# Flamingo layer on one Trainium2 core: combinations of x made from x before it is split, low parts of x on GpSimd, all value tiles ahead of the first query products

## The chip, the cores and the metric

The kernel runs on one core of a Trainium2 chip. The time is the device time of one execution in microseconds. A core has five engines, each with its own in-order queue: PE (TensorE), ACT (ScalarE), DVE (VectorE), POOL (GpSimd) and SP (SyncE, which here only issues DMAs). Each waits at an instruction until the semaphores that it names have reached their values.

## The reference, cut to what matters

Eight sequences of 128 tokens of width 512 and a context of the same shape go through two gated layers. The change concerns the first attention, with 32 heads of width 128:

```python
x = x + tanh(g_xattn[0]) * L0_xattn(layernorm(x), ctx, mask, bias, ln_weight, w_q, w_k, w_v, w_out)
...
xn = rmsnorm(hidden) * ln_weight
h_q, h_k, h_v = xn @ w_q.T, ctx @ w_k.T, ctx @ w_v.T
score = softmax(where(mask, h_q @ h_k.T + position_bias, -inf))
out = hidden + (score @ h_v) @ w_out.T
```

A linear layer, a second attention and an expert layer follow, which the change leaves alone.

## The kernel before

**Precision.** Every large product is made of three passes. A factor is split in a high part, rounded to the fast matmul type (fp32r), and a low part, which is the factor minus its high part; high times high, high times low and low times high are added up in PSUM. So each operand exists twice in SBUF. ACT writes the high part (`ACT.Copy` into an fp32r tile), DVE or POOL then subtracts it.

**Groups.** The 32 heads go in 8 groups of 4. Group 0 ("first") is written out by hand; groups 1 to 7 are a loop and a last body. In the loop, queries and keys are made by a Strassen-like scheme with seven products (`P1` to `P7`), which need *combinations* of the activations: T1, T2, T3 and N4, sums and differences of the blocks `x_block(i, s)` of x (i is the half of the width, s the half of the tokens) and of the same blocks `c_block` of the context. There are four combinations of each, every one split into high and low. They are made once, during group 0, in the tiles `work[0..3]`, written to DRAM (`combined`, by `put`), and fetched into a ring of places by the loop. Group 0 itself makes queries and keys plainly (`plain("q0a")`: head 0, tokens 0 to 511; `b`: the other half).

**Where x comes from.** DVE writes the normalised x (L1339). PE transposes it by sequence (`x_transposed`, L1861) into banks 4 to 7. Before the change ACT makes the high part out of PSUM, scaled by the norm weight, in four instructions of 128x128 for each sequence (`x_hi`, L964), and DVE the low part, again four (L1345). A combination of x is made from both parts of its blocks (`combine_x`, L1477, ten instructions of 128x1024 on DVE; `combine_context`, L1453, seven on DVE, and L663, three on POOL). `combined_hi` (ACT, L978) and `combined_lo` (POOL, L673) split each one. Combinations of the context come first, those of x after them, between softmax work.

**The order of the work.** Each engine's block is a list written by hand. PE's list in group 0, after the first keys, is: values 0 to 2 (`value`, L1937), x_transposed 0 to 3, value 3, x_transposed 4 to 7, the four query products of heads 0 and 1 (L1897), `scores` of head 0 (L1954), values 4 to 7, scores of head 1, keys of heads 2 and 3, `attend(0, 0)` (L1970), queries q2a, q2b, q3a, `attend(0, 1)`, q3b, scores of head 2, output projections (`project`, L1998). `UNITS` numbers all these tiles of work; four PSUM banks are given round by that number, so a tile waits until the one four places earlier has been emptied.

**The softmax** of a head runs DVE, ACT, DVE: `softmax_in` adds `bm` (made by POOL's `biasmask`, L682) to the scores in PSUM and takes the negative maximum (L1374, L1376), `exps` on ACT (L952), `softmax_out` scales and transposes (L1396, L1400). `scores` of head 1 waits until L1396 of head 0 has read each bank. SP then sends the turned probabilities to DRAM (`passed`) and back (`back`, into `keyed`), and `attend` waits for that. SP's DMAs stand in one queue.

`plain_hi` (ACT) and `plain_lo` (POOL) split the weights of the plain products; `plain_out` (ACT, L893) and `value_out` (ACT, L945) empty banks. `scores` of head 0 waits for `plain_out("q0b")`. L1352 to L1359 on DVE make the scaled x in `acc`, to which the outputs are added.

## Time and profile before

| | |
|---|---|
| median of 3 runs | 959.33 us (958.12 to 960.22) |
| profiled execution, its own time | 959.01 us |
| its span in the profile | 957.2 us |
| PE busy | 941.9 us, 98% of the span |
| DVE, ACT, POOL busy | 594.2, 399.5, 497.3 us |
| chain that ended last | PE 78%, DVE 8%, DMA 7% |

The profiled execution lies 0.3 us under the median. "Busy" is the time with an instruction on the engine. PE is busy nearly all the time, so time can only be won or lost where PE stands still, and group 0 takes the first 135 us of the span.

### The profile page before, as it was taken

The numbers are of one execution on the slowest core, as the hardware profiler recorded it, in microseconds if no ns is written. First come the engines' busy times: TensorE is split into PE (matmuls) and PEld (weight loads), VectorE is DVE, ScalarE is ACT, GpSimd is POOL, SyncE is SP. The second block draws the span as 40 slices with busy tenths as digits, with TensorE's granted clock in tenths as the row PEclk, the third lists the DMA queues.
The fourth block names the chain that finished last, engine by engine and source line by source line (L and its number), as shares of the span: only waits on it lengthen the run. The fifth ranks groups of instructions, "written<-read, shape, count | busy, mean of one in ns | idle before, by whom it ended". The sixth has DMA issues, their size and how long they took to land.

```text
span 957.2 us, 15391 instructions
## 1 busy us (share of the span) xinstructions
PE 941.9 (98%) x4850; PEld 793.9 (83%) x4850; DVE 594.2 (62%) x1020; ACT 399.5 (42%) x1080; POOL 497.3 (52%) x463
## 2 busy tenths in 40 slices
PE   9999899999999999999999999999999999999998
PEld 8888688788888888888888888888888888888885
DVE  4888846385538553855486447654666966756754
ACT  5765424252434233433443333433443346646630
POOL 3756754454446453646374637463646336687530
PEclk9999999999999999999999999999999999999999
DMA  7145676775687567766777667767687665200002
GB/s 283 45 152 222 234 255 249 259 266 196 241 276 275 219 241 263 271 244 241 251 271 256 241 241 260 270 248 237 226 292 266 230 224 183 91 23 1 2 1 88
DMA packets 67380, 199.44 MB, mean 208 GB/s; under 512 B 8720, under 2 KB 21264, under 8 KB 66320
## 3 DMA queue, kind: packets, MB, share of 16 engines
q1 hardware_dynamic: 66336, 197.67, 57.4%
q10 hardware_dynamic: 1008, 1.32, 0.4%
q8 instruction: 19, 0.31, 0.1%
q14 instruction: 17, 0.14, 0.0%
HBM read 174.85 MB, written 24.12 MB: 208 GB/s over the span
## 4 chain that ended last, share of the span: by engine, by line
PE 78%; DVE 8%; DMA 7%; issue 2%; SPq 2%; ACT 1%; POOL 1%; DVEq 0%; ACTq 0%
PE bank L1921 23%; PE bank L1998 16%; PE bank L2102 10%; PE bank L1937 10%; DMA keyed<-passing 6%; PE bank L1970 6%; PE bank L1954 5%; PE bank L1897 3%; PE bank L2126 2%; DVE turned_blocks L1396 1%; SPq L442 1%; DVE kt L1436 1%; DVE turned_blocks L1400 1%; PE bank L1982 1%; PE bank L2255 1%
## 5 line engine op out<-in xcount | busy, mean ns | idle before, releaser
L1998 PE MATMUL bank<-wvo,ao 128*128 128x512 f32 x768 | 179.9, 391 | 0.7 <-issue 0.6
L1937 PE MATMUL bank<-wvo,ct 128*128 128x512 f32 x768 | 177.7, 390 | 0.0
L1998 PEld LDWEIGHTS bank<-wvo,ao 128*128 128x128 f32 x768 | 143.0, 188 | 30.1 <-issue 1.0
L1937 PEld LDWEIGHTS bank<-wvo,ct 128*128 128x128 f32 x768 | 143.5, 188 | 29.3
L603 POOL TENSOR_TENSOR wvo<-stage,wvo 128x512 fp32r<-128x512 f32 x64 | 85.4, 1357 | 148.4 <-ACT wvo L906 148.3
L1921 PE MATMUL bank<-ring,wkq 128*128 128x512 f32 x648 | 157.4, 390 | 0.0
L1921 PEld LDWEIGHTS bank<-ring,wkq 128*128 128x128 f32 x648 | 121.2, 188 | 25.1
L1414 DVE SCALAR_TENSOR_TENSOR acc<-bank,gated_rows,acc 128x512 f32<-128x512 f32 x128 | 93.2, 742 | 39.4 <-PE bank L1998 38.3
L952 ACT ACTIVATE bank<-bank,nmax 128x128 f32<-128x128 f32 x256 | 88.2, 351 | 55.6 <-DVE nmax L1376 55.6
L1405 DVE TENSOR_TENSOR ao<-bank,ao 128x512 fp32r<-128x512 f32 x64 | 43.9, 691 | 106.6 <-ACT ao L958 106.6
L1436 DVE TENSOR_TENSOR qt<-bank,qt 128x512 f32<-128x512 f32 x98 | 66.4, 690 | 57.4 <-PE bank L1921 56.0
L682 POOL TENSOR_TENSOR bm<-maskneg,bias 128x1024 f32<-128x1024 f32 x32 | 78.9, 2465 | 26.0 <-DVE bank L1374 26.0
L945 ACT ACTIVATE vals<-bank 128x512 f32<-128x512 f32 x64 | 38.4, 600 | 94.7 <-PE bank L1937 94.4
L623 POOL TENSOR_TENSOR wkq_raw<-stage 128x256 f32<-128x256 f32 x27 | 20.3, 754 | 110.7 <-PE bank L1921 102.2
L1436 DVE TENSOR_TENSOR kt<-bank,kt 128x512 f32<-128x512 f32 x91 | 60.4, 682 | 26.6 <-PE bank L1921 25.0
L958 ACT ACTIVATE ao<-bank 128x512 fp32r<-128x512 f32 x64 | 37.9, 599 | 80.7 <-PE bank L1970 79.0
L1970 PEld LDWEIGHTS bank<-keyed,vals 128*128 128x128 f32 x512 | 61.0, 191 | 12.7 <-DMA keyed<-passing 11.1
L1970 PE MATMUL bank<-keyed,vals 128*128 128x128 f32 x512 | 63.6, 277 | 5.7 <-DMA keyed<-passing 5.6
L1374 DVE TENSOR_TENSOR bank<-bank,bm 128x512 f32<-128x512 f32 x64 | 44.4, 694 | 37.3 <-PE bank L1954 36.4
L1921 PE MATMUL bank<-xb,wkq 128*128 128x512 f32 x252 | 65.5, 395 | 0.0
L649 POOL TENSOR_TENSOR wkq<-wkq_raw,wkq 128x1024 fp32r<-128x1024 f32 x27 | 65.2, 2414 | 0.0
L1954 PEld LDWEIGHTS bank<-kt,qt 128*128 128x128 f32 x512 | 62.1, 191 | 3.4 <-DVE turned_blocks L1396 0.9
(187 smaller groups left out, 1511.9 us busy)
## 6 DMA issues: line engine op xcount, KB each, us to landing
ring<-combined SPq DMA_DIRECT2D x216, 512.0 KB, 6.3
stage<-in_w SPq DMA_DIRECT2D x63, 512.0 KB, 4.2
passing<-turned_blocks SPq DMA_DIRECT2D x24, 512.0 KB, 2.9
keyed<-passing SPq DMA_DIRECT2D x96, 128.0 KB, 3.2
combined<-work SPq DMA_DIRECT2D x16, 512.0 KB, 3.6
xraw<-in_x SPq DMA_DIRECT2D x2, 1024.0 KB, 11.3
bias<-in_bias SPq DMA_DIRECT2D x8, 256.0 KB, 4.5
cs<-in_ctx SPq DMA_DIRECT2D x1, 2048.0 KB, 7.8
```

The costliest lines, as they stand in the source:

```text
L603: pool.tensor_tensor(wvo[:, 1, h, :], stage[:, vo_stage(g, m, c)[0], :], wvo[:, 0, h, :].bitcast(fp32), ALU.subtract).then_inc(s_vo_lo, 1)
L649: pool.tensor_tensor(wkq[:, 3:7, 1, :, :].rearrange("p k c d -> p k (c d)"), wkq_raw[:, 3:7, 1, :, :].rearrange("p k c d -> p k (c d)"), w ...
L682: pool.tensor_tensor(bm[:, :, :], maskneg[:, :, :], bias[:, h:h + 1, :].to_broadcast([P, B, P]), ALU.add).then_inc(s_bm, 1)
L952: act.activation(scores, scores, ACT.Exp, bias=nmax[:, b:b + 1], accum_out=esum[:, b:b + 1]).then_inc(s_exp, 1)
L1414: dve.scalar_tensor_tensor(out=acc[:, b, :], in0=bank[un_of[m][f"o{i}"] % RING if to is None else to][:, :], scalar=gated_rows[:, b:b + 1] ...
L1436: dve.tensor_tensor(dst, bank[un_of[m][f"{ADDED[step]}.{j}"] % RING][:, :], other, ALU.add).then_inc(s_add, 1)
L1921: mm = pe.matmul(bank[b][:, :], wkq[:, FACTOR[p], w, c, :], right(s), start=(c == 0 and w + s == 0), stop=(c == 1 and w == 1))
L1937: mm = pe.matmul(bank[un_of[m][u] % RING][:, :], ct[:, i, c, b * P:(b + 1) * P], wvo[:, j, c, :], start=(c == 0 and i + j == 0), stop=(c = ...
L1954: mm = pe.matmul(bank[4 + s][:, (b - 4 * s) * P:(b - 4 * s + 1) * P], qt[:, h % 2, b * P:(b + 1) * P], kt[:, h % 2, b * P:(b + 1) * P], st ...
L1970: mm = pe.matmul(bank[6 + s][:, (b - 4 * s) * P:(b - 4 * s + 1) * P], vals[:, b, h * P:(h + 1) * P], right, start=True, stop=True)
L1998: mm = pe.matmul(bank[to][:, :], ao[:, h, p, b * P:(b + 1) * P], wvo[:, j, 2 * pair + h, :], start=(h == 0 and p + j == 0), stop=(h == 1 a ...
L2102: mm = pe.matmul(bank[b][:, 0:n], left(i, c), right[:, j, c, :], start=(c == 0 and i + j == 0), stop=(c == KC - 1 and i == 1 and last))
```

## The change

**x.** DVE copies the transposed x times the norm weight whole, in fp32, into the place of the low part (`x_raw`; two instructions of 128x256 for each sequence). ACT makes the high part from it in SBUF. DVE makes the four combinations from the whole x, four instructions in place of ten, and the low parts of the first two of them; then POOL subtracts the high part in place, so that the block holds the low part (`x_lo`, four instructions of 128x1024). **Context.** Its ten instructions all stand on DVE; POOL's three are gone. Combinations of x now come first. **Order.** Values 4 to 7 stand ahead of the query products, whose first now waits for three `x_lo` and the third for all four. Keys of heads 2 and 3 stand before and after scores of head 1, q2a ahead of `attend(0, 0)`. The raw x is loaded into `acc` itself.

```diff
-MAKING = ["T1", "T2", "N4", "T3"]
+MAKING = {1: ["T1", "T3", "T2", "N4"], 0: ["T1", "T2", "N4", "T3"]}
+X_STEPS = 6
...
-UNITS = {"first": (PLAIN_UNITS[0:4] + VALUES[0:4] + PLAIN_UNITS[4:8] + VALUES[4:8] + PLAIN_UNITS[8:16] + OUTS[:B]
+UNITS = {"first": (PLAIN_UNITS[0:4] + VALUES + PLAIN_UNITS[4:16] + OUTS[:B]
                    + PLAIN_UNITS[16:20] + OUTS[B:]),
...
+    xb_raw = nc.alloc_sbuf_tensor_at("xb_raw", [P, 3, 2, 2, H], fp32, offset=xr_at)
+    x01_raw = nc.alloc_sbuf_tensor_at("x01_raw", [P, 2, 2, H], fp32, offset=ring_at)
+    def x_raw(i, s):
+        return x01_raw[:, 1, :, :] if (i, s) == (0, 1) else xb_raw[:, {(0, 0): 0, (1, 0): 1, (1, 1): 2}[i, s], 1, :, :]
...
+    xraw = acc
...
-                def put(z, i, w):
-                    t = MAKING[i]
-                    sp.wait_ge(s_comb_lo, 4 * z + i + 1)
+                def put(z, i):
+                    t = MAKING[z][i]
+                    if z == 1 and i < 2:
+                        sp.wait_ge(s_comb, 4 + i + 1)
+                    else:
+                        sp.wait_ge(s_comb_lo, (i - 1 if z == 1 else 2 + i + 1))
                     for c in range(2):
+                        sp.dma_start(combined[z, TS.index(t), c, :, :, :], work[i][:, c, :, :].bitcast(fp32)).then_inc(s_cin[4 * z + i], 16)
...
                 sp.wait_ge(s_plain_lo, 4)
                 load(0, "q2", 0)
+                for i in range(4):
+                    put(1, i)
+                put(0, 0)
+                put(0, 1)
                 sp.wait_ge(s_plain_lo, 6)
                 load(0, "o0", 1)
                 passed(0, 0)
+                put(0, 2)
                 back(0, "first", 0)
-                put(0, 0, 0)
-                put(0, 1, 1)
-                put(0, 2, 2)
+                put(0, 3)
                 passed(0, 1)
                 back(0, "first", 1)
-                put(0, 3, 3)
                 sp.wait_ge(s_vo_lo, 6)
...
+                def x_lo(i, s):
+                    pool.wait_ge(s_xhi, 2 * (HB * s + HB))
+                    pool.wait_ge(s_comb, {(0, 0): 1, (0, 1): 2, (1, 1): 3, (1, 0): 4}[i, s])
+                    pool.tensor_tensor(x_block(i, s)[:, 1, :, :], x_raw(i, s),
+                                       x_block(i, s)[:, 0, :, :].bitcast(fp32), ALU.subtract).then_inc(s_xlo, 1)
...
+                def combined_lo(z, i):
+                    pool.wait_ge(s_comb_hi, 4 * (1 - z) + i + 1)
                     if z == 1:
-                        pool.wait_ge(s_comb, 7 + (4, 6, 7, 10)[i])
+                        pool.wait_ge(s_comb, 4)
                     elif i < 2:
-                        pool.wait_ge(s_comb, (1, 3)[i])
+                        pool.wait_ge(s_comb, X_STEPS + (4, 6)[i])
+                    pool.tensor_tensor(work[i][:, :, 1, :], work_raw[i][:, :, 1, :],
+                                       work[i][:, :, 0, :].bitcast(fp32), ALU.subtract).then_inc(s_comb_lo, 1)
...
+                for i, s in ((0, 0), (0, 1), (1, 0), (1, 1)):
+                    x_lo(i, s)
+                combined_lo(1, 2)
+                combined_lo(1, 3)
                 plain_lo(4)
+                combined_lo(0, 0)
+                combined_lo(0, 1)
                 biasmask(0, 1)
                 plain_lo(5)
-                pool.wait_ge(s_comb, 4)
-                combined_lo(0, 0, 0)
-                combined_lo(0, 1, 1)
-                combined_lo(0, 2, 2)
+                combined_lo(0, 2)
                 plain_lo(6)
+                combined_lo(0, 3)
                 plain_lo(7)
-                combined_lo(0, 3, 3)
...
-                    act.wait_ge(s_xT, b + 1)
...
+                    act.wait_ge(s_xraw, B + 2 * b + 2)
+                    for i in range(2):
+                        t = slice(b % 4 * P, (b % 4 + 1) * P)
+                        act.activation(x_block(i, b // 4)[:, 0, :, t], x_raw(i, b // 4)[:, :, t], ACT.Copy).then_inc(s_xhi, 1)
+                def combined_hi(z, i):
+                    act.wait_ge(s_comb, i + 1 if z == 1 else X_STEPS + (3, 5, 7, 10)[i])
+                    act.activation(work[i][:, :, 0, :], work_raw[i][:, :, 1, :], ACT.Copy).then_inc(s_comb_hi, 1)
...
                 for b in range(4, B):
                     x_hi(b)
+                value_out(0, "first", 4)
+                combined_hi(1, 0)
+                combined_hi(1, 1)
+                value_out(0, "first", 5)
+                combined_hi(1, 2)
+                combined_hi(1, 3)
+                value_out(0, "first", 6)
                 plain_hi(4)
-                for u in ("q0a", "q1a", "q0b", "q1b"):
-                    plain_out(u)
-                combined_hi(0, 0, 0)
+                value_out(0, "first", 7)
+                plain_out("q0a")
+                plain_out("q1a")
+                combined_hi(0, 0)
+                plain_out("q0b")
+                combined_hi(0, 1)
+                plain_out("q1b")
+                plain_hi(5)
                 exps(0, 0, [0])
-                value_out(0, "first", 4)
+                plain_out("k2a")
                 exps(0, 0, [1])
-                plain_hi(5)
-                value_out(0, "first", 5)
-                value_out(0, "first", 6)
-                combined_hi(0, 1, 1)
-                value_out(0, "first", 7)
-                combined_hi(0, 2, 2)
+                combined_hi(0, 2)
+                plain_out("k2b")
                 plain_hi(6)
                 exps(0, 1, [0])
-                plain_out("k2a")
+                plain_out("k3a")
                 exps(0, 1, [1])
-                plain_out("k2b")
+                combined_hi(0, 3)
                 plain_hi(7)
                 vo_hi(0, "first", "o0")
                 vo_hi(0, "first", "o1")
-                plain_out("k3a")
                 plain_out("k3b")
-                combined_hi(0, 3, 3)
+                plain_out("q2a")
...
+                dve.wait_ge(s_const, 32)
                 for b in range(B):
-                    dve.wait_ge(s_xhi, b * KC + KC)
-                    for c in range(KC):
-                        dve.scalar_tensor_tensor(out=x_block(c // 2, b // 4)[:, 1, c % 2, b % 4 * P:(b % 4 + 1) * P],
-                                                 in0=bank[4 + b % 4][:, c * P:(c + 1) * P], scalar=cols[:, 0, c:c + 1],
-                                                 in1=x_block(c // 2, b // 4)[:, 0, c % 2, b % 4 * P:(b % 4 + 1) * P].bitcast(fp32),
-                                                 op0=ALU.mult, op1=ALU.subtract).then_inc(s_xlo, 1)
+                    dve.wait_ge(s_xT, b + 1)
+                    for i in range(2):
+                        dve.tensor_tensor(x_raw(i, b // 4)[:, :, b % 4 * P:(b % 4 + 1) * P],
+                                          bank[4 + b % 4][:, i * 256:i * 256 + 256].rearrange("p (c t) -> p c t", c=2),
+                                          cols[:, 0, 2 * i:2 * i + 2].unsqueeze(2).to_broadcast([P, 2, P]),
+                                          ALU.mult).then_inc(s_xraw, 1)
+                dve.wait_ge(s_xraw, B + 2 * B)
+                t1, t3, t2, n4 = (work_raw[w][:, :, 1, :] for w in range(4))
+                dve.tensor_tensor(t1, x_raw(0, 1), x_raw(0, 0), ALU.subtract).then_inc(s_comb, 1)
+                dve.tensor_tensor(t3, x_raw(1, 1), x_raw(0, 1), ALU.subtract).then_inc(s_comb, 1)
+                dve.wait_ge(s_comb, 1)
+                dve.tensor_tensor(t2, x_raw(1, 1), t1, ALU.subtract).then_inc(s_comb, 1)
+                dve.wait_ge(s_comb, 3)
+                dve.tensor_tensor(n4, x_raw(1, 0), t2, ALU.subtract).then_inc(s_comb, 1)
+                for i in range(2):
+                    dve.wait_ge(s_comb_hi, i + 1)
+                    dve.tensor_tensor(work[i][:, :, 1, :], work_raw[i][:, :, 1, :], work[i][:, :, 0, :].bitcast(fp32),
+                                      ALU.subtract).then_inc(s_comb, 1)
                 dve.tensor_reduce(gated_rows[:, :], maskf[:, :, :], AX, ALU.max).then_inc(s_mf, 1)
...
+                combine_context([0, 1, 2, 3, 4, 5, 6])
                 softmax_in(0, 0)
                 softmax_out(0, "first", 0, 0)
                 softmax_out(0, "first", 0, 1)
-                combine_context([0, 1, 2, 3])
+                combine_context([7, 8, 9])
                 softmax_in(0, 1)
                 softmax_out(0, "first", 1, 0)
                 softmax_out(0, "first", 1, 1)
-                combine_context([4, 5, 6])
                 ao_lo(0, 0)
-                combine_x([0, 1, 2, 3, 4])
                 ao_lo(0, 1)
                 softmax_in(0, 2)
...
-                        pe.wait_ge(s_xlo, (b - 3) * KC)
+                        pe.wait_ge(s_xraw, B + 2 * (b - 3))
...
                 for x in range(4, B):
                     x_transposed(x)
-                pe.wait_ge(s_xlo, 4 * KC)
-                plain("q0a")
-                plain("q1a")
-                pe.wait_ge(s_xlo, B * KC)
-                plain("q0b")
-                plain("q1b")
-                scores(0, "first", 0)
                 for b in range(4, B):
                     value(0, "first", b)
+                for s in range(2):
+                    pe.wait_ge(s_xlo, 3 + s)
+                    plain("q0" + "ab"[s])
+                    plain("q1" + "ab"[s])
+                scores(0, "first", 0)
+                plain("k2a")
+                plain("k2b")
                 scores(0, "first", 1)
-                for u in PLAIN_UNITS[8:12]:
-                    plain(u)
+                plain("k3a")
+                plain("k3b")
+                plain("q2a")
                 attend(0, 0)
-                plain("q2a")
                 plain("q2b")
```

The places at which the lists differ and of which the prediction speaks follow. In brackets stand the semaphores waited for.

DVE before, from the end of the low parts of x to the first softmax (`gated_rows`, `rscale`, `vsum`, `msq` are small tiles, `bank` the scores of head 0):

```order
L1345 SCALAR_TENSOR_TENSOR xb<-bank,cols,xb 128x128 x2
L1349 TENSOR_REDUCE gated_rows<-maskf 128x8
L1352 TENSOR_SCALAR rscale<-rstd,tg 128x8 [waits act_prep]
L1354 SCALAR_TENSOR_TENSOR vsum<-mv,rscale 128x8 [waits rms_steps]
L1356 TENSOR_SCALAR msq<-rscale 128x8
L1359 TENSOR_SCALAR acc<-xraw,msq,vsum 128x512 [waits rms_steps]
L1359 TENSOR_SCALAR acc<-xraw,msq,vsum 128x512 x7
L1362 TENSOR_SCALAR gated_rows<-gated_rows,tg 128x8 [waits mask_steps]
L1374 TENSOR_TENSOR bank<-bank,bm 128x512 [waits biasmask_done,scores_done,layernorm_x,mask_steps]
L1376 TENSOR_REDUCE nmax<-bank 128x4 [waits scores_read]
```

DVE after the change, from the last `x_raw` tile on; `work_raw_96` to `work_raw_99` are the whole combinations T1, T3, T2 and N4 of x, `ctx_hi` is the semaphore that now counts `x_raw`:

```order
L1347 TENSOR_TENSOR work_raw_96<-x_raw,xb_raw 128x2x512 [waits ctx_hi]
L1348 TENSOR_TENSOR work_raw_97<-xb_raw,x_raw 128x2x512
L1350 TENSOR_TENSOR work_raw_98<-xb_raw,work_raw_96 128x2x512 [waits combine_steps]
L1352 TENSOR_TENSOR work_raw_99<-xb_raw,work_raw_98 128x2x512 [waits combine_steps]
L1355 TENSOR_TENSOR work_92<-work_raw_96,work_92 128x2x512 [waits combined_hi]
L1355 TENSOR_TENSOR work_93<-work_raw_97,work_93 128x2x512 [waits combined_hi]
L1357 TENSOR_REDUCE gated_rows<-maskf 128x8
L1360 TENSOR_SCALAR rscale<-rstd,tg 128x8 [waits act_prep]
L1362 SCALAR_TENSOR_TENSOR vsum<-mv,rscale 128x8 [waits rms_steps]
L1364 TENSOR_SCALAR msq<-rscale 128x8
L1367 TENSOR_SCALAR acc<-acc,msq,vsum 128x512 [waits rms_steps]
L1367 TENSOR_SCALAR acc<-acc,msq,vsum 128x512 x7
```

And directly behind these, on DVE after the change, up to the first softmax (`ct` is the context; the `work_raw` tiles are used again):

```order
L1370 TENSOR_SCALAR gated_rows<-gated_rows,tg 128x8 [waits mask_steps]
L1461 TENSOR_TENSOR work_raw_96<-ct 128x2x512 [waits ctx_in4,layernorm_x,mask_steps]
L1461 TENSOR_TENSOR work_raw_96<-work_raw_96,ct 128x2x512 [waits combine_steps] x2
L1461 TENSOR_TENSOR work_raw_97<-ct,work_raw_96 128x2x512 [waits combine_steps,ctx_in5]
L1461 TENSOR_TENSOR work_raw_97<-work_raw_97,ct 128x2x512 [waits combine_steps]
L1461 TENSOR_TENSOR work_raw_98<-ct,work_raw_97 128x2x512 [waits combine_steps,ctx_in6]
L1461 TENSOR_TENSOR work_raw_98<-work_raw_98,ct 128x2x512 [waits combine_steps]
L1382 TENSOR_TENSOR bank<-bank,bm 128x512 [waits scores_done,biasmask_done]
```

Where L1349 came directly behind the low parts, six instructions of 128x1024 now stand before it, and seven more of the context between the scaled x and the first softmax.

ACT before and after, from the fifth weight split to the first exponential (`qt` is a query tile emptied, `work` a high part of a combination, `vals` a value tile):

```order
L886 ACTIVATE wplain<-stage 128x512 [waits plain_done,stage_in1]
L893 ACTIVATE qt<-bank 128x512 [waits plain_done] x4
L978 ACTIVATE work_91<-work_raw_95 128x2x512 [waits pool_prep]
L952 ACTIVATE bank,esum<-bank,nmax 128x128 [waits negmax_done]
L952 ACTIVATE bank,esum<-bank,nmax 128x128 x3
L945 ACTIVATE vals<-bank 128x512 [waits values_done]
```

```order
L946 ACTIVATE vals<-bank 128x512 [waits values_done]
L894 ACTIVATE qt<-bank 128x512 [waits plain_done] x2
L971 ACTIVATE work_92<-work_raw_96 128x2x512 [waits combine_steps]
L894 ACTIVATE qt<-bank 128x512 [waits plain_done]
L971 ACTIVATE work_93<-work_raw_97 128x2x512 [waits combine_steps]
L894 ACTIVATE qt<-bank 128x512 [waits plain_done]
L887 ACTIVATE wplain<-stage 128x512 [waits plain_done,stage_in1]
L953 ACTIVATE bank,esum<-bank,nmax 128x128 [waits negmax_done]
```

The four `qt` stood together; now the third and fourth each stand behind a high part of a context combination, which waits for DVE's `combine_steps`.

POOL before, from the first `bm`, and after the change, behind it (`xb` and `x_61` are blocks of x, `wplain` weights):

```order
L682 TENSOR_TENSOR bm<-maskneg,bias 128x1024 [waits scores_read,bias_in]
L663 TENSOR_TENSOR work_raw_95<-ct 128x2x512 [waits x_transposed]
L663 TENSOR_TENSOR work_raw_95<-work_raw_95,ct 128x2x512 [waits pool_prep] x2
L597 TENSOR_TENSOR wplain<-stage,wplain 128x512 [waits plain_weights_hi]
L682 TENSOR_TENSOR bm<-maskneg,bias 128x1024 [waits scores_read]
L597 TENSOR_TENSOR wplain<-stage,wplain 128x512 [waits plain_weights_hi]
```

```order
L675 TENSOR_TENSOR xb<-xb_raw,xb 128x1024 [waits combine_steps,x_hi]
L675 TENSOR_TENSOR x_61<-x_raw,x_61 128x1024 [waits combine_steps,x_hi]
L675 TENSOR_TENSOR xb<-xb_raw,xb 128x1024 [waits combine_steps,x_hi] x2
L686 TENSOR_TENSOR work_94<-work_raw_98,work_94 128x2x512 [waits combine_steps,combined_hi]
L686 TENSOR_TENSOR work_95<-work_raw_99,work_95 128x2x512 [waits combine_steps,combined_hi]
L609 TENSOR_TENSOR wplain<-stage,wplain 128x512 [waits plain_weights_hi]
L686 TENSOR_TENSOR work_92<-work_raw_96,work_92 128x2x512 [waits combine_steps,combined_hi]
```

Three instructions that read the context went; four `x_lo` and two low parts of x combinations stand in their place, and each waits for DVE's combining.

## Rows read from the trace of the kernel before

**Rows 1.** What PE waited for in the first 160 us: total, times, longest, in us.

```profile
PE bank L1982 <- DVE ao L1405: 2.3, 1, 2.3
PE bank L1970 <- DMA keyed<-passing: 1.1, 1, 1.1
...
PE bank L1954 <- DVE turned_blocks L1396: 0.7, 1, 0.7
```

**Rows 2.** The page's TensorE clock, granted tenths in 40 slices of the span.

```profile
PEclk9999999999999999999999999999999999999999
```

**Rows 3.** PE in order of time: start, us, line, operation, tiles, count, idle before.

```profile
31.28 1.91 PE L1861 MATMUL bank<-ident,craw 128*128 128x128 f32 x16
...
37.52 0.63 PE L1861 MATMUL bank<-ident,craw 128*128 128x128 f32 x4 [0.27 <-DVE xb L1345]
...
50.61 11.14 PE L1937 MATMUL bank<-wvo,ct 128*128 128x512 f32 x48
...
61.59 1.95 PE L1954 MATMUL bank<-kt,qt 128*128 128x128 f32 x16
...
63.29 11.14 PE L1897 MATMUL bank<-ct,wplain 128*128 128x512 f32 x48
...
84.26 1.95 PE L1970 MATMUL bank<-keyed,vals 128*128 128x128 f32 x16
...
90.85 8.42 PE L1998 MATMUL bank<-wvo,ao 128*128 128x512 f32 x36
...
108.69 2.05 PE L1970 MATMUL bank<-keyed,vals 128*128 128x128 f32 x16 [1.14 <-DMA keyed<-passing]
```

**Rows 4.** DVE in order of time: low parts of x, context and x combinations.

```profile
33.14 4.22 DVE L1345 SCALAR_TENSOR_TENSOR xb<-bank,cols,xb 128x128 fp32r<-128x128 f32 x16 [1.46 <-ACT xb L964]
...
61.17 1.23 DVE L1453 TENSOR_TENSOR work_raw<-work_raw,ct 128x1024 f32<-128x1024 f32 x1
...
78.24 1.84 DVE L1477 TENSOR_TENSOR work_raw<-x,xb 128x1024 f32<-128x1024 f32 x1
...
80.12 2.21 DVE L1477 TENSOR_TENSOR work_raw<-work_raw,x 128x1024 f32<-128x1024 f32 x1
...
82.36 2.22 DVE L1477 TENSOR_TENSOR work_raw<-work_raw,xb 128x1024 f32<-128x1024 f32 x1
```

**Rows 5.** POOL in order of time, beside the same stretches.

```profile
62.47 7.10 POOL L673 TENSOR_TENSOR work<-work_raw,work 128x1024 fp32r<-128x1024 f32 x3 [4.94 <-DVE work_raw L1453]
...
78.95 4.55 POOL L603 TENSOR_TENSOR wvo<-stage,wvo 128x512 fp32r<-128x512 f32 x2
...
83.45 3.37 POOL L682 TENSOR_TENSOR bm<-maskneg,bias 128x1024 f32<-128x1024 f32 x1
```

**Rows 6.** Line L1359, scaled x in acc on DVE: min/median/max ns.

```profile
L1359 DVE TENSOR_SCALAR acc<-xraw,msq,vsum x8: 531/536/1420, 45.7 to 49.8; 128x512 f32<-128x512 f32 x8
```

**Rows 7.** ACT: the high part of one combination.

```profile
49.60 1.05 ACT L978 ACTIVATE work<-work_raw 128x1024 fp32r<-128x1024 f32 x1
```

**Rows 8.** DVE: first softmax of head 0, first and last of its instructions.

```profile
50.53 0.70 DVE L1374 TENSOR_TENSOR bank<-bank,bm 128x512 f32<-128x512 f32 x1
...
53.75 0.69 DVE L1396 TENSOR_TENSOR turned_blocks<-bank,rinv 128x512 f32<-128x512 f32 x1
...
55.87 0.69 DVE L1396 TENSOR_TENSOR turned_blocks<-bank,rinv 128x512 f32<-128x512 f32 x1
...
56.59 0.71 DVE L1400 STREAM_TRANSPOSE turned_blocks<-turned_blocks 128x512 f32<-128x512 f32 x1
```

**Rows 9.** SP: probabilities of heads 0 and 2 out and back.

```profile
57.93 0.43 SPq L432 DMA_DIRECT2D passing<-turned_blocks  x1
...
62.99 2.52 SPq L442 DMA_DIRECT2D keyed<-passing  x4
...
101.63 0.32 SPq L432 DMA_DIRECT2D passing<-turned_blocks  x1
...
104.28 1.74 SPq L442 DMA_DIRECT2D keyed<-passing  x4
```

85 lines of the change are left out of this document (8 added, 77 removed).

## The prediction

> **What bounds the kernel now.** PE is busy for 98% of the span, so I first asked what PE waits for in group 0, the only part that the change touches. The waits of PE in the first 160 us [rows 1] are 2.3 us for `ao_lo` of head 2 ahead of the transposes, 1.1 us for its probabilities coming back, and 0.7 us for the softmax of head 2 ahead of `scores` of head 3. All lie behind 99 us. Ahead of them PE waits 0.27 us for a low part of x [rows 3]. So the change can win at most 2.3 + 1.1 + 0.7 + 0.3 = 4.4 us, or 4.6 with the issue time beside the last; whatever it loses, it loses by making PE stand still.
>
> Then I looked at what DVE and POOL do to each other. One DVE instruction with two SBUF operands of 128x1024 takes 1.23 us when POOL is idle (second of [rows 4]). From 78.24 us on, three such take 1.84, 2.21 and 2.22 us, while POOL's pair of 128x512 at 78.95 takes 4.55 us and its `bm` at 83.45 takes 3.37 us [rows 4, 5]. Undisturbed, POOL needs 7.10/3 = 2.37 us for 128x1024 [rows 5], about 1.3 us for half of it. The ends tell how they share: DVE's second instruction ends at 82.33, which is 80.12 + about 1.1 us of waiting for POOL's first half + 1.15 of its own; POOL's second half then ends at 83.50, 1.2 us behind. 4.55 = 2 x 1.28 + 2 waits of 1.0. **They take turns, one whole instruction each, and neither overlaps.** A scaled-x instruction of L1359 falls under it too: seven took about 0.53 us, one 1.42 us [rows 6]. Instructions that read scores or products from PSUM do not: POOL's three of 2.37 us at 62.47 [rows 5] ran through a softmax of DVE undelayed.
>
> On this the change bears hard: it puts six POOL instructions of 128x1024 and one of 128x512 beside DVE's combining and scaling, all ahead of the first softmax.
>
> **The change part by part**, against the profiled execution's 959.01 us (0.3 us under the median of 959.33).
>
> *PE up to the first query.* x is transposed from 31.28 us; four tiles take 1.67 us, value 3 2.74. Without the wait of 0.27 us and the like amount behind it, PE ends the transposes at 37.4 in place of 37.9: gain 0.5. Values 4 to 7 (10.98 us from 50.61 to 61.59 [rows 3]) now follow, to 48.4.
>
> *DVE's whole x.* Sixteen instructions of 128x256 from PSUM, a form that the trace lacks: above 4.22/16 = 0.26 us for 128x128 [rows 4], under 0.69 for 128x512 [rows 8]. I take 0.36, by size. The last four tiles come off PE from 36.5 to 37.7, so DVE ends at about 39.3 (38.4 and 42 at the bounds). ACT's high parts follow within 0.7 us.
>
> *DVE against POOL, by turns,* with 1.15 us for a DVE turn, 2.3 for a POOL turn of 128x1024, 1.25 for one of 128x512:
> - T1 39.4 to 40.6; T3 to 41.8 (it waits for nothing); `x_lo` 1 to 44.1; T2 to 45.2; `x_lo` 2 to 47.5; N4 to 48.7; DVE's first low part to 49.8; `x_lo` 3 to 52.1; second low part to 53.2; `x_lo` 4 to 55.5.
> - Small ones to 55.6; `combined_lo` of x to 57.9 and 60.3 with one scaled-x instruction between or behind; `plain_lo(4)` to 62; the rest of the eight, at 0.47 each, to 65.3 (the eight span 45.7 to 50.3 with 0.9 of waiting [rows 6]).
> - Context steps at 1.26 each (1.23 plus the semaphore): the third, T1, done at 69.3, the fourth at 70.6; then turns again with POOL's two low parts, the seventh done at 76.6, or 78.9 if POOL wins one draw.
>
> If POOL did not hold up DVE, the same DVE list would end its third context step at 56.0 and its seventh at 61.
>
> *What PE loses by it.* First, q0a needs `x_lo` 3: 52.1 against 48.4, **3.7**. The four query products (10.9 us) end at 63.0; the fourth `x_lo` is in time. Second, `scores` of head 0 needs `plain_out("q0b")`, which on ACT stands behind `combined_hi(0, 0)`; that waits for the third context step, 69.3, takes 1.0 [rows 7], and the copy 0.5: 70.9, **7.9**. With scores (1.70) and k2a, k2b (5.45) PE is at 78.1. Third, `scores` of head 1 waits until L1396 of head 0 has read each bank. From `softmax_in` to these ends are 3.9 and 6.0 us (50.53 to 54.44 and 56.56 [rows 8]), so 80.5 and 82.6: **2.4** and **1.3**. PE leaves scores 1 at 83.5. Fourth, head 0's softmax ends 6.8 us behind its start [rows 8], 83.3; T3 of the context takes three DVE turns beside two of POOL's, to 89.8; softmax of head 1 starts there; its exponentials end near 94.9 (5.1 us in, ahead of the second L1396), and only then ACT splits T3 (95.8), POOL its low part (98.2) and the weights of q3 (99.5). PE, through k3a, k3b, q2a, `attend(0, 0)` and q2b, stands at q3a at 96.1 or, with head 0's probabilities late by a us, 97.4; it starts at 99.5: **2 to 3.4**. Fifth, SP sends head 1's probabilities behind `put(0, 3)`, at 99.0. A round trip took 7.1 us with nothing in front (101.63 to PE's start at 108.69), but 5.1 rather than 2.7 to the second half with a load in front (57.93 to 62.99) [rows 3, 9]. I take 5.2 + 4.4: PE starts `attend(0, 1)` at 108.6; it was ready at 102.3. **6.3**, or 3.8 with the short trip.
>
> Before, `attend(0, 1)` started at 84.26 [rows 3]: 24.3 us later. From there PE's list is the same as before; the projections, which began at 90.85 [rows 3], follow. The five combining instructions of x that stood between the softmax of heads 2 and 3 are gone from DVE and their halves from ACT and POOL, so the waits of 2.3, 1.1 and 0.7 us should go [rows 1]: -4.1. SP's fetches for the loop come as early as before, counted from there, and the loop is untouched. Sum: 24.3 - 4.1 = 20.2; 959.0 + 20.2 = **979.2**.
>
> The Trainium skill (SBUF — State Buffer, "Who interferes with whom") names `tensor_scalar` among the operations that can take both port pairs, if operands allow. The trace has it in one instruction of eight. If the eight did not wait, DVE's chain would be 4 us shorter and the sum 975.
>
> **The rivals.**
> 1. *No turns: the lists run as the durations say.* For it: not one row of before has DVE in the new `x_raw` form, and `x_lo` writes in place. Against it: rows 4 and 5. Then `x_lo` 3 is done at 47, the third context step at 56.0, PE waits nowhere up to q2b. SP still sends head 1's probabilities only at 80.7. With the long trip PE waits 6.4 for `attend(0, 1)`, starting it at 90.3 in place of 84.26, and ends at 959.0 + 6.0 - 4.1 = 961; with the short one at 958.4; if they come back by 83.5, when PE is ready, only the gains are left: 959.0 - 0.5 - 4.1 = 954.4. It decides where `x_lo` 3 ends before 48.4.
> 2. *The turns hold, but the queues behind them clear.* The first three losses stand (15.3 in all), head 1 comes in time: 959.0 + 15.3 - 0.5 - 4.1 = 969.7. For it: that part rests on the longest chain of my estimates.
> 3. *PE's clock falls after the long waits.* The granted clock shows 9 tenths or more in all 40 slices, with no wait over 2.3 us [rows 1, 2]; here are waits of 8 and 6 us. At 1.2 in place of 2.4 GHz, 128x512 at 0.23 us (10.98/48) would take twice that. Behind the 7.9 us the next wait swallows it; behind the last one `attend` and q3b (4.4 us) would be paid twice: 979.2 + 4.4 = 983.6. The Trainium skill (TensorE: Matmul & The Clock Gate) says that waits between bursts of matmuls can let the clock fall; no row here shows it.
>
> **How the numbers follow.** Forecast, 971 to 982 (the draw on POOL's side adds 2.3; the short trip, the undelayed scaling and the smaller `x_raw` take off 2.5, 4 and 1): 0.60. Rival 2, with the same spread, 963 to 971: 0.22. Rival 3: 0.05. Rival 1: 0.13, of which 0.07 under 957.1, 0.04 within 0.2% (957.4 to 961.2, about what a measurement can tell from no change), 0.02 above. So faster 0.08, same 0.04, slower 0.88. The range that holds 8 in 10 leaves out rival 1 and reaches up to rival 3: 963 to 984.
>
> **What would show it.** Right: on DVE, T2, N4 and the second low part at about 3.4 us each; PE waiting 3 to 4 us ahead of q0a for `x_lo`, and about 8 ahead of the first scores for ACT's q0b; the first softmax at 75 to 79 us; no wait ahead of the transposes of head 2. Wrong: DVE's combinations at 1.2 us beside `x_lo`; or PE at q0a by 48.5; or the losses there and the end at 960, which would mean that a later stage gives them back.

## The result and the profile after

| | before | after |
|---|---|---|
| median | 958.73 us (957.88 to 960.22, 4 runs) | 979.48 us (978.57 to 980.24, 4 runs) |
| profiled execution, its span | 959.01, 957.2 us | 980.24, 978.3 us |
| mean granted clock | 1.0 | 0.989 |
| PE, DVE, ACT, POOL busy | 941.9, 594.2, 399.5, 497.3 us | 949.9, 596.0, 395.8, 494.3 us |

The ratio is 1.0208 (95%: 1.0191 to 1.0226): slower by 20.7 us. The forecast was 979.2. DVE and POOL are busy for as long as before, though DVE has 17 instructions less (1003 for 1020) and the loop is the same. An instruction that waits for its turn counts as busy, and the rows below show that what the combinations save goes into such waits.

The waits of PE in the first 180 us of the kernel after, which answer to [rows 1]:

```profile
PE bank L1947 <- DMA keyed<-passing: 6.9, 2, 4.7
PE bank L1931 <- ACT qt L894: 5.2, 1, 5.2
PE bank L1874 <- POOL xb L675: 3.1, 1, 3.1
PE bank L1931 <- DVE turned_blocks L1404: 1.1, 2, 0.7
...
PE bank L1959 <- DVE ao L1413: 0.2, 1, 0.2
```

L1947 is `attend`, L1931 `scores`, L1874 the plain products, L1959 the transposes. The old waits of 2.3, 1.1 and 0.7 us have shrunk to 0.2; new ones of 16.3 stand ahead of them. PE's timeline, against [rows 3]:

```profile
37.54 11.13 PE L1914 MATMUL bank<-wvo,ct 128*128 128x512 f32 x48
51.72 7.36 PE L1874 MATMUL bank<-xb,wplain 128*128 128x512 f32 x24 [3.05 <-POOL xb L675]
...
69.72 3.57 PE L1931 MATMUL bank<-kt,qt 128*128 128x128 f32 x16 [5.20 <-ACT qt L894]
73.04 5.73 PE L1874 MATMUL bank<-ct,wplain 128*128 128x512 f32 x24
79.20 1.13 PE L1931 MATMUL bank<-kt,qt 128*128 128x128 f32 x8 [0.43 <-DVE turned_blocks L1404]
80.99 1.16 PE L1931 MATMUL bank<-kt,qt 128*128 128x128 f32 x8 [0.67 <-DVE turned_blocks L1404]
...
92.54 3.02 PE L1947 MATMUL bank<-keyed,vals 128*128 128x128 f32 x16 [2.19 <-DMA keyed<-passing]
...
106.41 3.79 PE L1947 MATMUL bank<-keyed,vals 128*128 128x128 f32 x16 [4.71 <-DMA keyed<-passing]
109.85 1.94 PE L1874 MATMUL bank<-x,wplain 128*128 128x512 f32 x6
...
114.71 8.42 PE L1975 MATMUL bank<-wvo,ao 128*128 128x512 f32 x36
...
154.32 1.52 PE L1898 MATMUL bank<-xb,wkq 128*128 128x512 f32 x6
```

Read as a ledger against before: `attend(0, 1)` starts at 106.41 in place of 84.26 (+22.15), the projections at 114.71 in place of 90.85 (+23.9), the loop at 154.32 in place of 135.06 (+19.3), and the span is 21.1 longer. So 22.15 are lost ahead of `attend(0, 1)`, 1.7 in it and in the work up to the projections, 4.6 come back behind it, and 1.8 are lost from the loop to the end. Of the 22.15, 16.3 are the waits above; the other 6 or so are PE's own work, which runs at the lower clock behind some of them (the first 24 query matmuls take 7.36 us, before 5.73). The 1.8 are no more than that stretch scatters by itself: from the start of the loop to the end, the traces of all kernels of this document but the last one take 819.4 to 824.0 us, before 822.1 and after 824.0.

DVE from the end of x_raw to the first softmax (L1347 T1, L1348 T3, L1350 T2, L1352 N4, L1355 two low parts, L1367 the scaled x, L1461 context steps, L1382 `softmax_in`):

```profile
39.28 1.23 DVE L1347 TENSOR_TENSOR work_raw<-x_raw,xb_raw 128x1024 f32<-128x1024 f32 x1
40.43 1.22 DVE L1348 TENSOR_TENSOR work_raw<-xb_raw,x_raw 128x1024 f32<-128x1024 f32 x1
41.56 3.43 DVE L1350 TENSOR_TENSOR work_raw<-xb_raw,work_raw 128x1024 f32<-128x1024 f32 x1
45.02 3.31 DVE L1352 TENSOR_TENSOR work_raw<-xb_raw,work_raw 128x1024 f32<-128x1024 f32 x1
48.26 4.49 DVE L1355 TENSOR_TENSOR work<-work_raw,work 128x1024 fp32r<-128x1024 f32 x2
...
53.80 1.20 DVE L1360 TENSOR_SCALAR rscale<-rstd,tg 128x8 f32<-128x8 f32 x1
55.04 2.31 DVE L1362 SCALAR_TENSOR_TENSOR vsum<-mv,rscale 128x8 f32<-128x8 f32 x1
...
57.47 6.70 DVE L1367 TENSOR_SCALAR acc<-acc,msq,vsum 128x512 f32<-128x512 f32 x8
...
65.60 2.49 DVE L1461 TENSOR_TENSOR work_raw<-work_raw,ct 128x1024 f32<-128x1024 f32 x2
...
70.78 3.20 DVE L1461 TENSOR_TENSOR work_raw<-ct,work_raw 128x1024 f32<-128x1024 f32 x1
...
75.16 0.69 DVE L1382 TENSOR_TENSOR bank<-bank,bm 128x512 f32<-128x512 f32 x1
```

and POOL beside it (L675 `x_lo`, L686 `combined_lo`):

```profile
40.65 3.25 POOL L675 TENSOR_TENSOR xb<-xb_raw,xb 128x1024 fp32r<-128x1024 f32 x1 [3.37 <-DVE work_raw L1347]
43.86 3.40 POOL L675 TENSOR_TENSOR x<-x_raw,x 128x1024 fp32r<-128x1024 f32 x1
48.48 6.50 POOL L675 TENSOR_TENSOR xb<-xb_raw,xb 128x1024 fp32r<-128x1024 f32 x2 [1.23 <-DVE work_raw L1352]
54.94 4.74 POOL L686 TENSOR_TENSOR work<-work_raw,work 128x1024 fp32r<-128x1024 f32 x2
```

The rows show the turns: T1 and T3 at 1.2 us each, T2 and N4 at 3.43 and 3.31, a low part at about 1.2 and the next at 3.3. `x_lo` takes 3.25 to 3.40 where POOL needs 2.37 alone [rows 5].

### The profile page after: what moved, and what is told of

It is laid out like the page before. It is cut to its first block, busy times and chain, and to the rows that moved or that the text cites. A ratio compares the mean times of both kernels' runs of the same rounds, so it can differ in the third digit from the quotient of the medians.

```text
span 978.3 us, 15359 instructions
## 1 busy us (share of the span) xinstructions
PE 949.9 (97%) x4850; PEld 800.7 (82%) x4850; DVE 596.0 (61%) x1003; ACT 395.8 (40%) x1064; POOL 494.3 (51%) x462
## 4 chain that ended last, share of the span: by engine, by line
PE 74%; DMA 8%; DVE 7%; issue 2%; SPq 2%; ACT 1%; POOL 0%; DVEq 0%; ACTq 0%
PE bank L1898 23%; PE bank L1975 15%; PE bank L2080 10%; PE bank L1914 9%; PE bank L1947 6%; DMA keyed<-passing 6%; PE bank L1931 5%; PE bank L2104 2%; DVE work_raw L1461 1%; SPq L456 1%; DMA passing<-turned_blocks 1%; DVE turned_blocks L1404 1%; DVE kt L1444 1%; DVE turned_blocks L1408 1%; PE bank L1874 1%
## 5 line engine op out<-in xcount | busy, mean ns | idle before, releaser
L615 POOL TENSOR_TENSOR wvo<-stage,wvo 128x512 fp32r<-128x512 f32 x64 | 82.1, 1303 | 167.1 <-ACT wvo L907 167.1
L695 POOL TENSOR_TENSOR bm<-maskneg,bias 128x1024 f32<-128x1024 f32 x32 | 76.8, 2401 | 20.2 <-DVE bank L1382 20.2
L1947 PEld LDWEIGHTS bank<-keyed,vals 128*128 128x128 f32 x512 | 63.9, 199 | 18.7 <-DMA keyed<-passing 17.0
L1947 PE MATMUL bank<-keyed,vals 128*128 128x128 f32 x512 | 66.7, 286 | 12.1 <-DMA keyed<-passing 11.8
L1931 PEld LDWEIGHTS bank<-kt,qt 128*128 128x128 f32 x512 | 63.5, 196 | 9.7 <-ACT qt L894 5.6
L1931 PE MATMUL bank<-kt,qt 128*128 128x128 f32 x512 | 64.2, 279 | 6.3 <-ACT qt L894 5.2
L1382 DVE TENSOR_TENSOR bank<-bank,bm 128x512 f32<-128x512 f32 x64 | 44.4, 694 | 38.7 <-PE bank L1931 37.7
```

Source lines behind the costliest of these rows:

```text
L615: pool.tensor_tensor(wvo[:, 1, h, :], stage[:, vo_stage(g, m, c)[0], :], wvo[:, 0, h, :].bitcast(fp32), ALU.subtract).then_inc(s_vo_lo, 1)
L695: pool.tensor_tensor(bm[:, :, :], maskneg[:, :, :], bias[:, h:h + 1, :].to_broadcast([P, B, P]), ALU.add).then_inc(s_bm, 1)
L1382: dve.tensor_tensor(scores, scores, bm[:, bs, :], ALU.add).then_inc(s_sadd, 1)
L1931: mm = pe.matmul(bank[4 + s][:, (b - 4 * s) * P:(b - 4 * s + 1) * P], qt[:, h % 2, b * P:(b + 1) * P], kt[:, h % 2, b * P:(b + 1) * P], st ...
L1947: mm = pe.matmul(bank[6 + s][:, (b - 4 * s) * P:(b - 4 * s + 1) * P], vals[:, b, h * P:(h + 1) * P], right, start=True, stop=True)
```

## The experiments

Twelve kernels. "Ratio" is to the kernel before, run on the same chip, with its 95% interval; the kernel after has 1.0208 (1.0191 to 1.0226).

**Does POOL's reading hold up DVE?** In place of four subtractions POOL sets the low parts of x to zero:

```diff
-                    pool.tensor_tensor(x_block(i, s)[:, 1, :, :], x_raw(i, s),
-                                       x_block(i, s)[:, 0, :, :].bitcast(fp32), ALU.subtract).then_inc(s_xlo, 1)
+                    pool.memset(x_block(i, s)[:, 1, :, :].bitcast(fp32), 0.0).then_inc(s_xlo, 1)
```

> The four x_lo subtractions on POOL are replaced by four instructions of POOL that set the low part of x to zero: they write the same tiles and read nothing. This leaves the low part of x out of the query products of group 0 and of the loop. Theory (what DVE takes turns with is POOL's reading of two SBUF operands): T2, N4 and the second low part on DVE take about 1.2 us each in place of 3.3 to 3.4, q0a does not wait, the first softmax starts at about 66 in place of 75.2 us, and the time is 968 to 971. Rival A (any POOL instruction of 128x1024 on SBUF takes a turn, one that only writes as well): DVE's rows stay near 3 us or fall only by what POOL's instruction is shorter, 974 to 978. Rival B (DVE's chain is not what bounds the end): the first softmax is earlier but the time stays above 977.

Measured: 969.9 us, ratio 1.0110 (1.0088 to 1.0132). DVE and POOL of this run:

```profile
42.01 1.22 DVE L1349 TENSOR_TENSOR work_raw<-xb_raw,work_raw 128x1024 f32<-128x1024 f32 x1
43.27 1.22 DVE L1351 TENSOR_TENSOR work_raw<-xb_raw,work_raw 128x1024 f32<-128x1024 f32 x1
...
67.14 0.69 DVE L1381 TENSOR_TENSOR bank<-bank,bm 128x512 f32<-128x512 f32 x1
```

```profile
41.08 0.96 POOL L675 MEMSET xb<- 128x1024 f32 x1 [3.83 <-DVE work_raw L1346]
42.22 0.96 POOL L675 MEMSET x<- 128x1024 f32 x1 [0.18 <-DVE work_raw L1347]
```

T2 runs from 42.01 to 43.23 with POOL's write of 42.22 to 43.18 inside it, and takes 1.22 us. So a POOL instruction that writes the same amount but reads nothing takes no turn, and the first softmax starts 8 us earlier. So what stretched T2 and N4, and with them DVE's list, is that POOL reads. The Trainium skill (SBUF — State Buffer, "Who interferes with whom") says that a DVE instruction with two SBUF inputs contends with a GpSimd instruction that reads SBUF and not with one that only writes; the run agrees.

**Who should make the low parts?** The four subtractions go to DVE, behind N4:

```diff
-                for i, s in ((0, 0), (0, 1), (1, 0), (1, 1)):
-                    x_lo(i, s)
...
+                for i, s in ((0, 0), (0, 1), (1, 0), (1, 1)):
+                    if s == 0 and i:
+                        dve.wait_ge(s_comb, 4)
+                    dve.tensor_tensor(x_block(i, s)[:, 1, :, :], x_raw(i, s),
+                                      x_block(i, s)[:, 0, :, :].bitcast(fp32), ALU.subtract).then_inc(s_xlo, 1)
```

> One part of the change undone: the four low parts of x are made by DVE, behind N4 and ahead of its first combined low part, and not by POOL. Theory (DVE's list with the turns sets the first softmax; one instruction of DVE costs it 1.2 us, one of POOL that takes a turn costs DVE 2.2, but POOL's two combined low parts now come beside the four): the wait of 3.1 us ahead of q0a shrinks to 0 to 1.5, the first softmax still starts at 74 to 76 us, PE waits by so much longer ahead of the scores, and the time stays at 978 to 980. Rival (the wait ahead of q0a counts in full): 976 to 977.

Measured: 975.48 us, ratio 1.0159 (1.0136 to 1.0182): 4.0 us less than after, 4.7 by the ratios, whose intervals do not meet. I had not expected that, and it is not the rival's way either, for q0a waits 3.15 us, as in the kernel after. DVE of this run:

```profile
57.51 0.22 DVE L1364 TENSOR_SCALAR rscale<-rstd,tg 128x8 f32<-128x8 f32 x1
57.76 0.17 DVE L1366 SCALAR_TENSOR_TENSOR vsum<-mv,rscale 128x8 f32<-128x8 f32 x1
...
58.05 3.74 DVE L1371 TENSOR_SCALAR acc<-acc,msq,vsum 128x512 f32<-128x512 f32 x8
...
72.81 0.69 DVE L1386 TENSOR_TENSOR bank<-bank,bm 128x512 f32<-128x512 f32 x1
```

DVE takes on four instructions (4.9 us of its own), and its first softmax still starts 2.35 us earlier. The gain lies in rows that I had held to be small: with POOL silent after 53 us, rscale and vsum, 8 columns each, take 0.22 and 0.17 us where they took 1.20 and 2.31, and the eight scalings 3.74 where they took 6.70. These are 6.1 us of pure waiting in the kernel after; the list ahead of them is 3.6 us longer (from T1 to rscale 18.07 us for 14.52), not 4.9, since the turns fall otherwise there too. A turn costs what is left of POOL's instruction, here up to 2.1 us, however small DVE's own is; the forecast gave the small ones 0.1 us behind the fourth `x_lo`. It also answers the question left open beside rows 6: the eight `tensor_scalar` do wait.

**Do ACT's and SP's places matter?** Two edits of the kernel after. In the first ACT copies q0b, q1b and splits a weight ahead of the first context combinations:

```diff
-                combined_hi(0, 0)
                 plain_out("q0b")
-                combined_hi(0, 1)
                 plain_out("q1b")
                 plain_hi(5)
+                combined_hi(0, 0)
+                combined_hi(0, 1)
```

> Change alone: on ACT, the copies of q0b and q1b and plain_hi(5) stand ahead of the high parts of the first two context combinations. Theory (DVE's list, stretched by the turns with POOL, sets when the first softmax can run; ACT's order only decides where PE waits for it): PE starts the scores of head 0 at about 64.6 us in place of 69.7, and stands still by as much longer ahead of the scores of head 1 or of k2, because the first softmax still starts at about 75 us; the time stays within 1.5 us of the changed kernel's 979.5. Rival (the place of the high parts on ACT is itself the cost): the wait of 5.2 us goes and nothing takes its place, 974 to 975.

Measured: 978.9 us, 1.0195 (1.0176 to 1.0215), no difference from after that the intervals show. PE's wait of 5.20 is gone and one of 9.06 is in its place:

```profile
52.44 5.73 PE L1874 MATMUL bank<-xb,wplain 128*128 128x512 f32 x24 [3.05 <-POOL xb L675]
...
63.45 1.95 PE L1931 MATMUL bank<-kt,qt 128*128 128x128 f32 x16
...
79.91 3.87 PE L1931 MATMUL bank<-kt,qt 128*128 128x128 f32 x16 [9.06 <-DVE turned_blocks L1404]
```

So the 5.2 us that PE's list lays on ACT are DVE's: the last releaser in a row is not always the cause. In the second SP sends head 1's probabilities first:

```diff
-                put(0, 3)
                 passed(0, 1)
+                put(0, 3)
```

> Change alone: SP sends the probabilities of head 1 ahead of the last context combination. Theory (the round trip starts late and is long because the send stands behind two DMAs of 0.5 MB): the probabilities leave at about 94.5 in place of 97.05 us, the trip takes about 7 in place of 9.4 us, and attend(0, 1) starts 2.5 to 4.7 us earlier: 975 to 977. Rival (the trip is not lengthened by what stands ahead of it, or PE only waits elsewhere instead, for the low part that q3a needs): under 1 us, 978.5 to 979.5.

Measured: 976.92 us, 1.0170 (1.0143 to 1.0196). The wait is 3.22 in place of 4.71, `attend(0, 1)` starts at 103.99 in place of 106.41 and the projections at 111.96 in place of 114.71. The time is as forecast, but single runs spread from 973.5 to 978.4, and the interval just touches that of after. The reason given for it held only in half: the probabilities leave at 94.72 in place of 97.05, but their trip takes 9.3 us as before and not 7, for the two stores of the combination now stand between the way out and the way back. What is won is the earlier start alone.

**What does PE's clock cost?** Matmuls whose result nobody reads fill PE's four waits:

```diff
+                def fill(n):
+                    for _ in range(n):
+                        pe.matmul(bank[7][:, 0:P], ident[:, :], ident[:, :], start=True, stop=True)
```

> Adds matmuls of 128x128 whose result nobody reads (12, 20, 7 and 18) in the places where PE waits for the low parts of x, for the scores of head 0, for attend(0, 0) and for attend(0, 1); every wait of the changed kernel stays. Theory (part of the loss is that PE works at the lower granted clock behind its waits): the granted clock stays at 1.00 through the first 120 us, attend(0, 1) with q3b takes 6.1 in place of 8.3 us, and the time falls by 2 to 3 us, to 976.5 to 977.5; what the other stretches at the lower clock cost is hidden by the waits behind them. Rival (the lower clock is hidden by waits everywhere): 979.5, or later by what the added matmuls hold up.

Measured: 977.05 us, 1.0179 (1.0157 to 1.0200), mean clock 1.0 in place of 0.989. First the kernel after, the clock by stretches of 5 us (columns: stretch, length, PE busy, PEclk, DMA share, GB/s):

```profile
50.00:55.00 5.00, 3.28 (x9) 0.75 0.80 325
...
105.00:110.00 5.00, 3.59 (x17) 0.50 0.60 211
200.00:205.00 5.00, 3.78 (x20) 0.76 0.06 18
```

then PE of the run with the filling:

```profile
52.00 5.74 PE L1874 MATMUL bank<-xb,wplain 128*128 128x512 f32 x24 [0.39 <-POOL xb L675]
...
106.35 2.05 PE L1947 MATMUL bank<-keyed,vals 128*128 128x128 f32 x16 [1.46 <-DMA keyed<-passing]
```

The same 24 query matmuls take 5.74 us in place of 7.36, `attend(0, 1)` 2.05 in place of 3.79. `attend(0, 1)` starts at the same time as in after (106.35 and 106.41), so what the lower clock cost ahead of it, the 6 us of the ledger, would otherwise have been waits; the projections start 2.0 us earlier. The median is 2.4 us shorter, 2.8 by the ratios, whose intervals just overlap.

**The two halves apart.** First the order alone, on the kernel before: values 4 to 7 ahead of q0a, keys around the scores of head 1, q2a ahead of `attend(0, 0)`:

```diff
+                for b in range(4, B):
+                    value(0, "first", b)
                 pe.wait_ge(s_xlo, 4 * KC)
                 plain("q0a")
...
                 scores(0, "first", 0)
-                for b in range(4, B):
-                    value(0, "first", b)
+                plain("k2a")
+                plain("k2b")
                 scores(0, "first", 1)
```

> The other part of the change alone, on the kernel before: values 4 to 7 ahead of the first queries, keys of heads 2 and 3 around the scores of head 1, q2a ahead of attend(0, 0), with ACT's list to match; x, its combinations, POOL, SP and DVE are as before. Theory (the order costs nearly nothing by itself: the low parts of x are ready 7 us ahead of q0a, and the first softmax starts at about 61 in place of 50.5, early enough for attend(0, 1)): 957 to 963. Rival (the later first softmax is what costs: the order alone has a good part of the 20 us): 966 or more.

Measured: 974.0 us, 1.0146 (1.0122 to 1.0169), as the rival had it. Its PE waits:

```profile
PE bank L1897 <- POOL wplain L597: 8.0, 1, 8.0
PE bank L1998 <- issue: 3.4, 1, 3.4
```

q2a waits for its weights, which stand on POOL behind three combinations that wait for the softmax of head 0, now 11 us later. I took that for a mere misplacement in a second kernel, and put POOL's `plain_lo(6)` ahead of the combinations and SP's `passed(0, 1)` ahead of their `put`:

```diff
+                plain_lo(6)
                 combined_lo(0, 0, 0)
                 combined_lo(0, 1, 1)
                 combined_lo(0, 2, 2)
-                plain_lo(6)
```

> The order alone on the kernel before, once more, with two places of the other queues put right: POOL makes the low part of q2's weights ahead of the three context combinations, and SP sends head 1's probabilities ahead of those combinations. Theory (what the order alone cost was 8.0 us for q2's weights behind POOL's 7.0 us of combinations, and what followed from it; the rest is that the 11 us of values no longer cover the two softmaxes and the round trip): the wait ahead of q2a falls to 1 to 3 us, a wait of 2 to 5 us for the probabilities of head 1 appears, and the time is 963 to 969. Rival (the lost cover alone makes up the loss, so the wait only moves): 972 to 975.

Measured: 971.25 us, 1.0123 (1.0100 to 1.0145), between both forecasts. The 8.0 us fall to 4.4, in two waits that are again for POOL's weights and not for probabilities, but the 3.4 ahead of the projections rise to 5.2. There DVE's `ao_lo` of head 1 starts at 103.25, directly behind five x steps, and the first of these had waited 2.66 us for stores of combinations that this edit had put behind head 1's probabilities. So misplaced queues still had a share, and no kernel here has the order alone with all of them put right: 12.7 us is what the order cost in this form, not the least that it can cost. Now the x part alone: values 4 to 7 back between the scores.

```diff
-                for b in range(4, B):
-                    value(0, "first", b)
                 for s in range(2):
                     pe.wait_ge(s_xlo, 3 + s)
...
                 scores(0, "first", 0)
+                for b in range(4, B):
+                    value(0, "first", b)
+                scores(0, "first", 1)
                 plain("k2a")
                 plain("k2b")
-                scores(0, "first", 1)
```

> The changed kernel with values 4 to 7 put back between the scores of heads 0 and 1, and ACT's list to match: the x part of the change alone, in about the order of before. Theory (the lists of DVE and POOL and the probabilities' round trip set when attend(0, 1) can start, whatever PE does ahead of it): q0a waits for the third low part from about 37.5 to 51.7 us (14 us), the scores of head 0 wait again until about 69.7, values 4 to 7 fill the time behind them, attend(0, 1) starts at 105 to 107.5 as in the changed kernel (106.4), and the time is 976 to 981. Rival (the two parts add up): the order alone cost 14 of 20.7 us, so x alone costs 6 to 7: 964 to 967.

Measured: 976.29 us, 1.0181 (1.0157 to 1.0205). As the theory had it:

```profile
51.90 7.53 PE L1874 MATMUL bank<-xb,wplain 128*128 128x512 f32 x24 [13.84 <-POOL xb L675]
...
69.89 3.42 PE L1931 MATMUL bank<-kt,qt 128*128 128x128 f32 x16 [5.02 <-ACT qt L894]
...
107.29 2.05 PE L1947 MATMUL bank<-keyed,vals 128*128 128x128 f32 x16 [0.40 <-DMA keyed<-passing]
```

PE works 11 us less ahead of q0a and waits 11 us more; the scores of head 0 start at 69.89 against 69.72, `attend(0, 1)` at 107.29 against 106.41. The x part costs 17.8 us and the order 14.0 (12.7 with two queues put right), each against the before of its runs, and 20.7 together: they do not add, since both delay the same thing, the scores of head 0 (48.91 before, 60.24 with the order, 69.89 with x, 69.72 with both).

**Can another order save it?** The kernel after, with six context steps, softmax of head 0, four scalings, softmax of head 1, then the rest on DVE; ACT, POOL and SP put combinations behind what PE waits for:

```diff
-                combine_context([0, 1, 2, 3, 4, 5, 6])
+                combine_context([0, 1, 2, 3, 4, 5])
                 softmax_in(0, 0)
...
-                combine_context([7, 8, 9])
+                scaled(range(4))
                 softmax_in(0, 1)
...
+                combine_context([6, 7, 8, 9])
+                scaled(range(4, B))
```

> The changed kernel with the same instructions in another order: on DVE the softmax of heads 0 and 1 no longer stands behind the scaling of x and the last context combinations (six of the ten context steps, softmax of head 0, four scalings, softmax of head 1, the other context steps, four scalings); ACT and POOL make the context's high and low parts behind what PE waits for; SP sends probabilities ahead of combinations. Theory (the turns are a price that only counts where the softmax stands behind them): PE starts the scores of head 0 at about 65 us, the first softmax starts at 65 to 67, attend(0, 1) at 88 to 91; the waits ahead of it come to 5 to 7 us with the 3.1 ahead of q0a, and the time is 957 to 962. Rival (the turns themselves fill the time, in whatever order): above 968.

Measured: 972.66 us, 1.0133 (1.0111 to 1.0155). A miss. The scores of head 0 start at 66.03, as said, but the first softmax only at 70.91 (forecast 65 to 67), behind the six context steps, two of which still take turns, and `attend(0, 1)` at 99.77 in place of 88 to 91. PE waits 11.1 us up to there, not 5 to 7, and the last of these waits is for DVE's `ao_lo`, which the new order itself put behind four context steps and four scalings. With, on top, the low parts of x in another order:

```diff
-MAKING = {1: ["T1", "T3", "T2", "N4"], 0: ["T1", "T2", "N4", "T3"]}
+MAKING = {1: ["T1", "T2", "N4", "T3"], 0: ["T1", "T2", "N4", "T3"]}
...
-                    pe.wait_ge(s_xlo, 3 + s)
+                    pe.wait_ge(s_xlo, 2 + 2 * s)
```

> The kernel with the list in another order, as above, and the four combinations and low parts of x in the order T1, T2, N4, T3 and (0, 0), (1, 0), (0, 1), (1, 1), so that q0a needs two low parts and not three. Theory: the second low part ends at about 47.5 us, ahead of value 7's end at 48.4 us; the wait ahead of q0a (3.1 us) goes, and as the softmax no longer bounds, the time falls by as much: 954.5 to 958, at or below the kernel before. Rival (DVE's list still bounds the scores of head 0): the wait only moves, within 1 us of the run before it.

Measured: 971.63 us, 1.0126 (1.0103 to 1.0149), within 1.1 us of the run before it: the rival. The wait ahead of q0a is gone, and one of 6.6 us stands ahead of the scores of head 1. PE of the two runs, first without, then with the other order of the low parts:

```profile
66.03 1.95 PE L1935 MATMUL bank<-kt,qt 128*128 128x128 f32 x16
...
99.77 2.02 PE L1951 MATMUL bank<-keyed,vals 128*128 128x128 f32 x16 [2.22 <-DVE ao L1414]
```

```profile
61.70 1.95 PE L1935 MATMUL bank<-kt,qt 128*128 128x128 f32 x16
...
75.69 3.60 PE L1935 MATMUL bank<-kt,qt 128*128 128x128 f32 x16 [6.59 <-DVE turned_blocks L1405]
...
100.55 2.02 PE L1951 MATMUL bank<-keyed,vals 128*128 128x128 f32 x16 [2.35 <-DVE ao L1414]
```

What these runs have in common is the time from the scores of head 0 to `attend(0, 1)`, worked out from the PE rows, beside what of it PE waited. It does not order the times, which also hang on when it starts and on what comes behind.

| kernel | scores(0) at | attend(0, 1) at | between | of it waiting | values in between |
|---|---|---|---|---|---|
| before | 48.91 | 84.26 | 35.4 | 0 | yes |
| order alone | 60.24 | 95.43 | 35.2 | 8.0 | no |
| order alone, two queues put right | 61.30 | 92.35 | 31.0 | 4.4 | no |
| x alone | 69.89 | 107.29 | 37.4 | 0.4 | yes |
| after | 69.72 | 106.41 | 36.7 | 8.0 | no |
| after, reordered | 66.03 | 99.77 | 33.7 | 8.1 | no |
| the same, low parts too | 61.70 | 100.55 | 38.9 | 11.9 | no |

The stretch takes 31 to 39 us in every kernel, with values 4 to 7 in it or without. PE's own work there is 35.4 us with the values and 24.4 without (35.4 less their 10.98); what the waits do not account for beyond that is PE at the lower clock. Before, the values covered the chain of two softmaxes, a round trip and the combinations between them with little to spare: the last load of head 1's probabilities was issued at 77.8 and such loads landed 2.6 to 3.4 us later, so about 3 us ahead of 84.26. An estimate from these numbers: a chain of 32 us that starts 11 us later, at 60.24, ends at 92, where PE without the values would be ready at 84.6, 7 to 8 us sooner. The order alone waited 8.0, though for POOL's weights and thus at another link of the chain. So whoever moves the values ahead starts the chain later and takes its cover away. They do fill PE's wait for the low parts, but that wait exists only since the change.

**Can before be bettered by what was learnt?** Two tries at its waits of 2.3, 1.1 and 0.7 us. The first moved three x steps of DVE behind parts of the softmaxes of heads 2 and 3, the second moved two of them further, behind `ao_lo(0, 2)`, where DVE idled. The second edit:

```diff
-                combine_x([6])
                 softmax_out(0, "first", 2, 1)
                 add_out(0, "first", 3)
-                combine_x([7])
+                combine_x([6])
                 add_out(0, "first", 4)
-                combine_x([8])
                 add_out(0, "first", 5)
-                combine_x([9])
                 softmax_in(0, 3)
+                combine_x([7])
...
                 ao_lo(0, 2)
+                combine_x([8, 9])
                 ao_lo(0, 3)
```

> The kernel before, changed only between the softmaxes of heads 2 and 3, where its three PE waits lie (2.3, 1.1 and 0.7 us): DVE makes a step of the x combinations behind and not ahead of the second half of head 2's softmax, two more steps behind and not ahead of softmax_in of head 3, and ACT empties k4a and attend(0, 2) ahead of the last combination and of two weights. Theory (combination steps of x ahead of the softmax are what these waits are made of): 2 to 3.5 us faster than before. Rival (the combinations, later by 1 to 3 us, reach the loop's fetches late, and the loop pays): 0, or slower.

> The kernel before once more, with the x combinations taken off the way of the softmax of head 3 and of the transposes behind it: DVE makes the seventh step behind head 2's softmax, the eighth behind softmax_in of head 3, the last two behind ao_lo of head 2, where it was idle for 5 us; all additions to acc keep their places; ACT and POOL make the last high and low parts behind k4b and the weights. Theory (in group 0 DVE's list is the second bound, so PE's three waits shrink only if DVE has less ahead of ao_lo of head 2, and the last run moved too little off it and made additions late): the wait of 2.3 us ahead of the transposes falls under 1, those of 1.1 and 0.7 us go, and the loop's fetches at about 124 in place of 118 us are still in time: 2 to 4 us faster. Rival (the combinations take turns with POOL wherever they stand, or the loop's first ring tiles come late): within 1 us of before, or slower.

Measured: 958.56 us, 1.0002 (0.9988 to 1.0016), and 963.64 us, 1.0034 (1.0015 to 1.0052). The first is no different from before; the second is 3 to 4 us slower, and its interval lies above 1. In the first the waits only changed places (1.8 for `ao_lo`, 1.7 and 0.9 for additions to `acc` that came late). In the second they went, all but 1.2 us, and the loop began at 131.33 in place of 135.06. Then:

```profile
139.88 2.33 PE L1920 MATMUL bank<-ring,wkq 128*128 128x512 f32 x9 [2.95 <-ACT qt L931]
145.25 1.65 PE L1920 MATMUL bank<-ring,wkq 128*128 128x512 f32 x3 [3.04 <-DMA ring<-combined]
```

The loop's first products caught up with SP's queue: the combinations are fetched from 125.2 us on in place of 118.2, and a load of weights behind them comes so late that ACT waits 13.2 us for it, to 138.20, ahead of emptying PE's banks. From there to the end the kernel takes 829.1 us, before 822.1. I read this as the other side of the change: combinations of x made early let group 0's end run free, and in before they have a due time that cannot move by 7 us. No version here beats before; whether another order of the x part could is open.

## Why the prediction was right, step by step

The time and the mechanism were right, the close hit was in part luck: errors of 2 to 4 us cancelled.

- **Turns, whole instruction each.** Right. T2 3.43 and N4 3.31 us (about 3.4 forecast), and the zeroing run shows the cause. x_raw, forecast to end at 39.3 with 0.36 us each, ended at 39.25 with 0.41 at a pitch of 0.33. The third context step ended at 68.1 (69.3), the first softmax started at 75.16 (76.6): each a little early, though the small rows, which waited for POOL too, ended 1.8 us later than forecast (57.4 for 55.6). The eight scalings made up for it: they took 6.70 us where the forecast had 9.7, and the context steps behind them went as forecast.
- **First loss,** q0a: 3.05 (3.7). **Second,** the scores of head 0: 5.20 (7.9), as the third step was 1.2 us early and as the queries ran 1.9 us longer at the lower clock. **Third,** the scores of head 1: 0.43 and 0.67 (2.4 and 1.3). **Fourth,** the low part for q3a: none (2 to 3.4); instead `attend(0, 0)` waited 2.19 for the probabilities of head 0, which the prediction had "late by a us". The forecast had all of the loss as waits, about 25 us less a gain of 0.5; measured were 16.3 us of waits and some 6 of slower work, which the run with filled waits shows to be the same time in another form. **Fifth,** `attend(0, 1)`: 4.71 (6.3). The round trip took 97.05 to 106.41, 9.4 us, where I took 9.6 and put it at 99.0. So `attend(0, 1)` came at 106.41 and not at 108.6: the steps ahead of it were 2.2 us too dear together.
- **Gains.** 4.6 us between the projections and the loop (4.1 forecast), and the waits of 2.3, 1.1 and 0.7 went as said.
- **Rival 3, the lower clock, came true as a mechanism, and not with its cost.** The forecast had nothing for it and held it at 0.05. The clock did fall behind the waits: 1.7 us are lost for it behind `attend(0, 1)`, where the rival had 4.4. In the loop before's wait of 1.7 us at a head's probabilities left the clock at 1.00 and after's of 2.34 took it to 0.76 in the stretch of 200 to 205 us; that fits the 1.8 lost there, which is within the scatter.
- **Luck.** The forecast of 979.2 met 979.5 because 2.2 us too much ahead of `attend(0, 1)` and 3.5 too little behind it nearly cancel (gains 0.5 better). In the chances, rival 1's 0.02 above belongs with the slower ones, which makes 0.89 and leaves 0.07 for faster, not 0.88 and 0.08.
- **Rivals 1 and 2** fell: there were turns, and the queues behind them did not clear (`attend(0, 0)` and `attend(0, 1)` waited 6.9 us for probabilities).
- **The scalings wait,** so the case in which they did not, with a sum of 975, fell as well: the first two span 3.96 us beside POOL, and the eight 3.74 with POOL silent.

## What to carry to other kernels

An instruction moved from a busy engine to an idle one need not save anything where the two exclude each other: here four subtractions of 2.4 us on POOL cost DVE more than the 1.2 us each that DVE needed for them. Ask of each stretch of PE work which chain of other engines it covers; before it is moved, compare the chain's length with the cover that stays. And where two changes delay the same start, test each alone: their costs do not add, and undoing one may give back little of the sum (by the ratios 3 us of the 20.7 with the order undone, and 6 to 8 with x undone).

## What was not expected of the hardware

- A DVE instruction of 8 columns waits for POOL's whole instruction too: 2.31 us in place of 0.17 for `scalar_tensor_tensor`, 1.20 in place of 0.22 for `tensor_scalar` with a column as its scalar.
- A write of 128x1024 by POOL ran wholly inside a subtraction of DVE, and neither took longer (0.96 and 1.22 us).
- PE's granted clock fell to the lower level, 1.2 in place of 2.4 GHz, behind waits of 2.19, 3.05, 4.71 and 5.20 us in the kernel after, and not behind one of 1.90 (the run with SP's order) or 1.71 (before). It is not a matter of the wait alone. With ACT's and with SP's order the wait ahead of q0a is 3.05 and 3.06 us as well, and the 24 query matmuls behind it take 5.73 and 5.78 us, full speed, where after has 7.36. In the reordered kernel a wait of 2.44 us left `attend` at 2.05 us. And in the first try to better before, behind waits of 0.93, 1.69 and at last 1.80 us within 14 us, twelve matmuls took 4.44 us in place of 3.01. No run here shows what decides. The Trainium skill (TensorE: Matmul & The Clock Gate) says that waits between bursts can let the clock fall; here the traces agree, with these numbers, and filling the waits with matmuls that nobody reads kept it at 1.00.
